# Four fused layers on one core: the last attention steps in a written order, retention's last row factor on GpSimd, the first rows by tile

## What is computed

```python
x = x + tanh(g_xattn[0]) * retention(ln(x), ctx, ctx)      # relu(x@wg) * groupnorm(...) @ wo
x = x + tanh(g_ffn[0])   * moe(ln(x))                      # top 2 of 8 experts + shared, gelu
x = x + tanh(g_xattn[1]) * attention(ln(x), ctx)           # fp8-rounded projections, self + context
x = x + tanh(g_ffn[1])   * dense(ln(x))
# dense:
shared_out = relu(x @ W_up.T) @ W_down.T
rw = softmax(top_k(x @ W_gate.T, 2))
out = shared_out + sum(rw) * (x @ W_expert)
```

## Time and profile before

| | |
|---|---|
| median of 3 executions | 1713.87 us (1713.71 to 1713.95) |
| the profiled execution | 1714.87 us, its span 1713.1 us |
| TensorE busy | 1630.4 us, 95% of the span |
| ScalarE, VectorE, GpSimd busy | 1102.9, 1081.3, 480.9 us |
| mean granted TensorE clock | 0.989 of full speed |
| DMA | 219.67 MB, mean 128 GB/s |

### The profile page before, as it was taken

How to read it: one execution, slowest core, us unless ns; L and a number is a source line. 1 busy time by engine, 2 the same in 40 slices (tenths; PEclk the granted TensorE clock), 3 DMA queues, 4 the chain that set the end, 5 groups by cost and what they waited for, 6 DMA issues and landing times.

```text
span 1713.1 us, 27138 instructions
## 1 busy us (share of the span) xinstructions
PE 1630.4 (95%) x9136; PEld 1337.7 (78%) x9136; DVE 1081.3 (63%) x2117; ACT 1102.9 (64%) x2974; POOL 480.9 (28%) x511
## 2 busy tenths in 40 slices
PE   6989779999998999999999999999999999998998
PEld 5888656666777778888788888788888788876887
DVE  6158854444876667777777776666666666786322
ACT  3454235543657888888888888878777878873100
POOL 1000122223424233433433433333443333420000
PEclk9999889999999999999999999999999999999999
DMA  6120649885663133364343353121151221100011
GB/s 242 49 80 34 266 138 315 299 287 168 235 237 125 50 127 145 113 265 164 113 152 130 127 225 117 57 86 55 56 233 56 69 79 55 56 25 1 25 37 37
DMA packets 74820, 219.67 MB, mean 128 GB/s; under 512 B 6288, under 2 KB 14480, under 8 KB 68304
## 3 DMA queue, kind: packets, MB, share of 16 engines
q1 hardware_dynamic: 69024, 199.56, 32.0%
q0 software_dynamic: 5680, 18.62, 3.5%
HBM read 157.60 MB, written 60.56 MB: 127 GB/s over the span
## 4 chain that ended last, share of the span: by engine, by line
PE 71%; ACT 5%; DVE 5%; DMA 4%; issue 1%; POOL 1%; another core or an unknown queue 0%; POOLq 0%; ACTq 0%; DVEq 0%
PE bank L2377 9%; PE bank L2378 9%; PE bank L97 7%; PE bank L98 7%; PE bank L99 7%; PE bank L2456 6%; PE bank L2438 6%; PE bank L2469 6%; PE bank L2427 5%; DMA s_rows<-x_rows,t_tok 4%; PE bank L2448 3%; PE bank L1349 3%; PE bank L1369 3%; ACT t_sc L2577 1%; ACT t_y L2615 1%
## 5 line engine op out<-in xcount | busy, mean ns | idle before, releaser
L2680 DVE TENSOR_TENSOR t_hn<-bank,t_rs 128x256 f32<-128x256 f32 (+1 forms) x256 | 130.8, 552 | 137.2 <-POOL t_rs L2342 70.4
L2377 PE MATMUL bank<-t_slot,t_x_q 128*128 128x512 f32 x512 | 205.5, 401 | 0.0
L2339 POOL TENSOR_SCALAR t_ve<-t_ss 128x4 f32<-128x4 f32 (+1 forms) x128 | 25.9, 202 | 628.6 <-DVE t_ss L2676 619.4
L2378 PE MATMUL bank<-t_slot,t_x_q 128*128 128x512 f32 x512 | 200.1, 391 | 0.0
L2577 ACT ACTIVATE t_sc<-bank,t_mx 128x128 f32<-128x128 f32 x512 | 183.9, 455 | 3.5 <-DVE t_mx L2700 3.5
L2342 POOL TENSOR_TENSOR t_rs<-t_ve,t_mhalf 128x4 f32<-128x4 f32 (+1 forms) x128 | 171.0, 1336 | 10.6
L2577 ACT ACTIVATION_READ_ACCUMULATOR t_sc<-bank,t_mx 128x1 f32 x512 | 151.6, 296 | 0.0
L2615 ACT ACTIVATE t_y<-bank,smooth 128x128 bf16<-128x128 f32 x512 | 139.2, 399 | 2.1 <-PE bank L2456 2.1
L2438 PEld LDWEIGHTS bank<-t_hT 128*128 128x128 f32 x1024 | 120.9, 192 | 15.8 <-ACT t_hT L2604 15.0
L2438 PE MATMUL bank<-t_hT 128*128 128x128 f32 x1024 | 131.4, 281 | 1.6 <-ACT t_hT L2604 1.6
L2377 PE MATMUL bank<-t_slot,t_x_kv 128*128 128x256 f32 x512 | 125.3, 283 | 2.1 <-DVE x_res L1647 1.4
(11 more groups left out here) (326 smaller groups left out, 4160.1 us busy)
## 6 DMA issues: line engine op xcount, KB each, us to landing
t_xh<-xq_scratch SPq DMA_DIRECT2D x64, 512.0 KB, 3.6
t_slot<-w_ready SPq DMA_DIRECT2D x16, 2048.0 KB, 8.4
t_cr<-in_ctxT_dram SPq DMA_DIRECT2D x64, 256.0 KB, 2.7
y_rows<-s_y SPq DMA_DIRECT2D x39, 256.0 KB
e_w<-in_w_units_dram SPq DMA_DIRECT2D x8, 1024.0 KB, 11.5
w_rows<-in_w_qkv_dram SPq DMA_DIRECT2D x8, 1024.0 KB, 7.2
w_ready<-w_hi SPq DMA_DIRECT2D x8, 1024.0 KB
w_ready<-w_lo SPq DMA_DIRECT2D x8, 1024.0 KB
```

The lines of the kernel that those rows point to most:

```text
L2377: nc.tensor.matmul(out, x_in[:, k, :], w[0][:, k, a:b], start=k == 0, stop=False)
L2378: last = nc.tensor.matmul(out, x_in[:, k, :], w[1][:, k, a:b], start=False, stop=k == KT - 1)
L2680: nc.vector.tensor_tensor(hn[:, lo:hi, :], b3[bk][:, 0:hi - lo, :], rs[:, lo:hi].unsqueeze(2).broadcast_to([P, hi - lo, P]), ALU.mult).the ...
```

## The change

Three parts.

**A.** Chunk 0 of x is loaded as four tiles with a semaphore each, ahead of the parameters; VectorE measures each tile as it lands; TensorE's first turn goes tile by tile instead of group by group; VectorE writes low(0) before statistics(1).

**B.** Three tiles of chunk 3 are measured before the last addition of retention; GpSimd makes the factor of chunk 3 as it does for the others; low(2) moves ahead of the barrier; the root and reciprocal behind it are gone.

**C.** `step` no longer carries Dense's pieces of steps 63 to 66 on TensorE, ScalarE and VectorE; each gets a `last_steps()` with everything written in one order. In `Dense.tensor` the first expert rows come ahead of logits(0), the second ahead of the turned logits(0), and only the second waits for the last row of x; VectorE's first four lines of `Dense.vector` move into `last_steps`.

```diff
-def tile_statistics(nc, env, dve, stats, count, tiles):
+def tile_statistics(nc, env, dve, stats, count, tiles, done=0):
-    for t in tiles:
+    for t in tiles[done:]:
         nc.vector.bn_stats(...)
...
 # Retention.sync
+        for j in range(J):
+            sp.dma_start(env.x_res[:, j, :], dram["x"][j]).then_inc(self.tile_in[j], 16)
         sp.dma_start(env.par[:], dram["params"]).then_inc(self.par_in, 16)
-        rows(0)
...
 # Retention.tensor
+        def first_turn():
+            for j in range(J):
+                pe.wait_ge(self.normed, j + 1)
+                for k in range(KT):
+                    last = nc.tensor.transpose(bank[k][:, ramp(j)], self.xn[0][:, j, ramp(k)], env.ident[:])
+                    if j == J - 1:
+                        last.then_inc(self.turned, 1)
-        turn(0)
+        first_turn()
...
 # Retention.vector
+                for j in range(J):
+                    dve.wait_ge(self.tile_in[j], 16)
+                    v.bn_stats(env.st[:, j, :], env.x_res[:, j, :]).then_inc(self.stats, 1)
...
+        low(0)
         statistics(1)
-        low(0)
         normalise(1)
...
 # Values.gpsimd
-        for c in range(C - 1):
+        for c in range(C):
             pool.wait_ge(self.final, (c + 1) * 2 * J)
             so.row_factors(pool, c)
 # Values.vector, projected(c)
+                if c == 3 and j == 2:
+                    dve.wait_ge(self.x_in, c * J + j + 1)
+                    for t in range(c * J, c * J + J - 1):
+                        v.bn_stats(env.st[:, t, :], env.x_res[:, t, :]).then_inc(self.final, 1)
...
+            if c == C - 1:
+                so.low(dve, 2)
 # Sorting.vector
-        v.tensor_scalar(self.var[:, 0:J], env.mv[:, last_rows, 1], LN_EPS, None, ALU.add).then_inc(self.var_in, 1)
-        dve.wait_ge(self.roots, 1)
-        v.reciprocal(env.rstd[:, last_rows], self.root[:, 0:J]).then_inc(self.rs_in, 1)
         self.normalise(dve, 3, range(J))
-        self.low(dve, 2)
...
 # Dense.expert
         if n == 0:
             pe.wait_ge(self.wlo, self.n["expert"])
+        if n == 1:
             pe.wait_ge(self.rows_in, Q * B)
 # Dense.tensor
+        self.expert(pe, 0, 0)
         self.logits(pe, 0)
-        self.expert(pe, 0, 0)
+        self.expert(pe, 0, 1)
         self.turn_logits(pe, 0)
-        self.expert(pe, 0, 1)
...
 # attention, tensor
+        def last_steps():
+            pe.wait_ge(n_in, M * 4 - 2)
+            de.turn(pe, 0, range(2))
+            turn_probs(M - 2)
+            output(M - 4, M % 2, M * 2 - 2, None)
+            de.turn(pe, 0, range(2, KT))
+            attend(M - 2, M % 2)
+            turn(M - 1)
+            de.turn(pe, 1, range(2))
+            scores(M - 1)
+            de.turn(pe, 1, range(2, KT))
+            de.up(pe, 0, 0)
+            de.up(pe, 0, 1)
+            turn_probs(M - 1)
+            output(M - 3, 1 - M % 2, M * 2, None)
+            attend(M - 1, 1 - M % 2)
+            de.up(pe, 0, 2)
+            output(M - 2, M % 2, M * 2, None)
+            de.up(pe, 0, 3)
+            de.turn(pe, 2, range(2))
+            output(M - 1, 1 - M % 2, M * 2, None)
+            de.turn(pe, 2, range(2, KT))
...
 # attention, scalar
+        def last_steps():
+            exps(M - 2)
+            squares_b(M - 1)
+            de.x_hi(act, 0, range(2))
+            probs_out(M - 2)
+            de.x_hi(act, 0, range(2, KT))
+            heads_out(M - 1)
+            de.x_hi(act, 1, range(2))
+            scaled_out(M - 2, None)
+            exps(M - 1)
+            de.relu(act, 0, 0)
+            de.x_hi(act, 1, range(2, KT))
+            de.relu(act, 0, 1)
+            probs_out(M - 1)
+            scaled_out(M - 1, None)
+            de.relu(act, 0, 2)
+            de.high(act, "expert", 0, KT)
+            de.relu(act, 0, 3)
...
 # attention, vector
+        def last_steps():
+            maxima(M - 2)
+            de.normalise(dve, 1, range(J))
+            probabilities(M - 2)
+            sums_b(M - 1)
+            de.x_lo(dve, 0, range(2))
+            rounded(M - 3, 1 - M % 2, 0)
+            normalise_b(M - 1)
+            de.x_lo(dve, 0, range(2, KT))
+            rounded(M - 3, 1 - M % 2, 1)
+            residual(M - 4, None)
+            de.x_lo(dve, 1, range(2))
+            maxima(M - 1)
+            de.statistics(dve, (10, 11))
+            de.aggregate(dve, 2)
+            probabilities(M - 1)
+            de.h_low(dve, 0, 0)
+            de.x_lo(dve, 1, range(2, KT))
+            rounded(M - 2, M % 2, 0)
+            de.h_low(dve, 0, 1)
+            rounded(M - 2, M % 2, 1)
+            residual(M - 3, None)
+            de.statistics(dve, (12, 13))
+            de.normalise(dve, 2, range(J))
+            rounded(M - 1, 1 - M % 2, 0)
+            de.h_low(dve, 0, 2)
+            rounded(M - 1, 1 - M % 2, 1)
+            residual(M - 2, None)
+            de.low(dve, "expert", 0, KT)
+            de.h_low(dve, 0, 3)
+            de.x_lo(dve, 2, range(2))
+            residual(M - 1, None)
+            de.x_lo(dve, 2, range(2, KT))
+            de.statistics(dve, (14, 15))
+            de.aggregate(dve, 3)
```

More of the change, by code:

```diff
@@ L871, in __init__ @@
         self.tiles = [sb(f"tiles{i}", [P, 4 + E]) for i in range(3)]
-        self.var, self.root, self.dif, self.e1, self.s1 = (sb(n, [P, B]) for n in ("var", "root", "dif", "e1", "s1"))
+        self.dif, self.e1, self.s1 = (sb(n, [P, B]) for n in ("dif", "e1", "s1"))
         self.graw, self.posf, self.slot, self.row, self.ids = (
@@ L889, in __init__ @@
         self.same, self.picked = mem.at("r_same", 170, [P, self.N, E]), mem.at("r_picked", 171.25, [P, self.N, E])
-        (self.wg_in, self.wg_hi, self.wg_lo, self.var_in, self.roots, self.normed, self.turned, self.hi_in, self.lo_in,
+        (self.wg_in, self.wg_hi, self.wg_lo, self.normed, self.turned, self.hi_in, self.lo_in,
          self.lps, self.lsb, self.tps, self.lg_in, self.dif_in, self.e1_in, self.made, self.pad_in, self.scan_in, self.sort_ps,
@@ L894, in __init__ @@
              ctx.enter_context(nc.semaphore("r_" + n)) for n in (
-                 "wg_in", "wg_hi", "wg_lo", "var_in", "roots", "normed", "turned", "hi_in", "lo_in", "lps", "lsb", "tps",
+                 "wg_in", "wg_hi", "wg_lo", "normed", "turned", "hi_in", "lo_in", "lps", "lsb", "tps",
                  "lg_in", "dif_in", "e1_in", "made", "pad_in", "scan_in", "sort_ps", "at_in", "b2_raw_in", "b2_hi_in",
@@ L1046, in scalar @@
         nc, env = self.nc, self.env
-        act.wait_ge(self.var_in, 1)
-        nc.scalar.activation(self.root[:, 0:J], self.var[:, 0:J], ACT.Sqrt).then_inc(self.roots, 1)
         def logits_out(c):
@@ L1889, in after_maxima @@
             self.aggregate(dve, 1)
-        if at == -1:
-            self.normalise(dve, 1, range(J))
     def after_residual(self, dve, at):
@@ L1905, in after_residual @@
             self.statistics(dve, (8, 9))
-        if at == -1:
-            self.x_lo(dve, 0, range(2, KT))
-            self.statistics(dve, (10, 11))
-            self.aggregate(dve, 2)
-            self.x_lo(dve, 1, range(2))
-        if at == 0:
-            self.statistics(dve, (12,))
-            self.h_low(dve, 0, 2)
-            self.h_low(dve, 0, 3)
-            self.normalise(dve, 2, range(J))
-        if at == 1:
-            self.statistics(dve, (13,))
-            self.x_lo(dve, 2, range(2))
-        if at == 2:
-            self.statistics(dve, (14,))
     def logits(self, pe, c):
@@ L2100, in vector @@
     def vector(self, dve):
-        self.statistics(dve, (15,))
-        self.aggregate(dve, 3)
-        self.x_lo(dve, 2, range(2, KT))
-        self.low(dve, "expert", 0, KT)
         self.normalise(dve, 3, range(J))
@@ L2202, in side, with steps @@
         return slice((1 - part) * QH, (1 - part) * QH + QH)
-    def steps(eng, step):
+    def steps(eng, step, end=M - 1):
         for i in range(B + FIRST):
@@ L2214, in steps @@
                     step(v * 2 + (first + 1), (FIRST + 1) % 2, quarter)
-            for i in range(first + 2 * loops, first + B):
+            for i in range(first + 2 * loops, min(first + B, end)):
                 step(i, i % 2, None)
@@ L2365, in gpsimd @@
         rstd(0, 0)
-        steps(pool, step)
+        steps(pool, step, M + FIRST)
         de.rstd(pool, 2)
@@ L2513, in tensor @@
         steps(pe, step)
+        last_steps()
         de.tensor(pe)
@@ L2620, in step @@
                 exps(i - 1)
-            if number(i) == M - 1:
-                de.x_hi(act, 0, range(2))
-            if number(i) == M:
-                de.x_hi(act, 1, range(2, KT))
-                de.relu(act, 0, 0)
             if has(i):
@@ L2632, in step @@
                 probs_out(i - 1)
-            if number(i) == M - 1:
-                de.x_hi(act, 0, range(2, KT))
-            if number(i) == M:
-                de.relu(act, 0, 1)
             if has(i):
@@ L2644, in step @@
                 scaled_out(i - 1, quarter)
-            if number(i) == M - 1:
```

(12 more changed lines are left out.)

42 lines of the change are left out of this document (12 added, 30 removed).

## The result

The changed kernel takes 1695.63 us (1692.54 to 1699.67, 4 executions) against 1713.91 us for the kernel before on the same chip (1713.71 to 1717.81): a ratio of 0.9889, 95% interval 0.9864 to 0.9915, or 19.0 us less where 14.5 were forecast. It is faster, as forecast. But 0.9889 of the first median is 1694.9, and the range ended at 1695.0: the gain was 0.1 us larger than the range allowed. The profiled execution is the shortest of the four, 1692.54 us with a span of 1690.8 us.

A forecast was written before the change was run, and what follows sets the result against it. TensorE, nearly always busy, was taken as the bound, gaining only where it waits or runs slowly, mainly start and tail. Profiled 1714.87 minus 3.6 plus 0.1 minus 11.0 gives 1700.4; less 1.0 to the median, 1699.4 us; range 1695.0 to 1704.5.

The forecast's parts named there:

- rival 2: Start: TensorE's full clock comes early and stays, so the start gains 2 us more, 1697.4 in all; chance 0.14.
- Rival 3: Start: split loads land one after another (1702.0), or low halves stick behind GpSimd's operation (1702.8); chance 0.12.
- the table load: Start: ScalarE loads the root's table in 1.28 us, costing 0.6, with no added drain of about 1.38.
- the two forecast: Tail: new TensorE waits of 0.7 us each, for ScalarE's heads at scores(63) and VectorE's first low half of chunk 3.
- the term for TensorE's busy time: Tail: half clock loses 3.3 us, of which 3.0 counted as winnable because a part coincides with waiting.
- its bound of 12.0: Tail: the most the new order of the last steps was expected to gain, in us; the lower bound was 8.0.
- my two ways of working it out: Tail gain: 11.8 us of waits and clock less 1.4 gives 10.4; walking the lists gives 11.6; middle taken, 11.0.
- the walk through the lists: Tail: five instruction lists, each instruction at its measured length; turn(3) 12.3 us earlier, less 0.7, gives 11.6.
- Rival 1: Tail: VectorE becomes the bound, with 33.6 us of work in 39; 3 us lost, 1702.4 in all; chance 0.18.
- rival 5: Tail: now without gaps, it is granted half clock; slower beyond 29 us of it, 1722 at 45; chance 0.03.
- the last sentence of the sum: Middle of the kernel: the start's gain passes through undiminished, as every wait there is on something that shifts too.
- the 11.0 of C: Tail: forecast gain in us from reordering the last steps, the middle between 10.4 and 11.6.

The follow-up runs named there:

- after: The changed kernel with all three parts, first measurement and profile, against the kernel before: 1695.63 us, ratio 0.9889.
- after_again: The changed kernel run once more with nothing altered: 1696.14 us, ratio 0.9900 to the kernel before.
- part_a: The kernel before with only the change to the first rows at the start: 1707.09 us, ratio 0.9965 to the kernel before.
- old_vector: The changed kernel with VectorE alone back in its old order in the last steps: 1711.22 us, ratio 0.9994 to the kernel before.
- old_tensor: The changed kernel with TensorE alone in its old order in the last steps and Dense's first chunk: 1704.16 us, ratio 0.9951 to the kernel before.
- extra_copies: The changed kernel plus 15 unread 1 MB DRAM copies issued by SyncE in the routed stage: 1721.63 us, ratio 1.0049 to the kernel before.
- best: The changed kernel with first-chunk projections each waiting only for their own low half, and three Dense.tensor pieces moved later: 1692.97 us, ratio 0.9880 to the kernel before.
- staggered: best with prepared weights' low half stored a slot after the high half and next rows loaded a slot later: 1688.77 us, ratio 0.9877 to the kernel before.
- part_b: The kernel before with only the change at retention's end: 1712.32 us, ratio 1.0001 to the kernel before.
- one_load: The changed kernel with its first four tiles in one 1 MB load instead of four: 1696.05 us, ratio 0.9901 to the kernel before.

## Why the prediction was right, and where it was wrong

**Part A was right in size, in part by luck.** The forecast had tiles at 3.5 to 6.5, the parameters at 6.9, rows from 8.85, the projection at 16.05; measured are 3.61 to about 6.25, 6.44, 8.41 and 15.81. One link of the chain was wrong. The transposed weights came at 7.10, not 7.67, and the turn ended at 12.46, not 13.4, but ScalarE was not free then: it had waited for `wg` to land. In all six profiles with this start the projection follows the start of that weight split by 5.1 to 5.3 us. The early steps and the late `wg` nearly cancelled. Over the profiles, the first projection is at 19.60 in the four kernels with the old start and at 16.26 in the six with the new one as it is (after, after_again, part_a, old_vector, old_tensor, extra_copies), and the scan begins at 207.49 and 203.84 in the mean: 3.65 us for A, with 3.6 forecast. The scan of the six lies between 202.76 and 205.85, so this is good to about 1 us, and the first pair's 4.97 is at the upper end. Of rival 2 a little is true. In after the full clock did come at the turn's end, at about 12.0, but went back to half at 15.4, until 18.9. The first twelve products took 4.25 us where they took 4.98 before, and in the mean of the profiles 4.6 in the six and 4.8 in the four: 0.2 us, not 2. Only in best and staggered, whose first projection starts at 14.08 and 13.48, did the full clock stay.

**Rival 3 did not come.** The low halves ran at their normal 0.62 us each beside `wg_lo`, and four loads landed like one: the last of four tiles was there by 6.25, where its statistics start, and one load of all four at 6.18. The Trainium skill ("DMA: Bandwidth & Descriptors", Rules for kernel authors) would have many small transfers coalesced. In this case neither is shown to be better: four loads of 256 KB landed like one of 1 MB, put the load of `wg` 1.3 us later into the queue, and the scan begins as early either way. Of the table load, this trace agrees with the one before and not with the page: the root starts at 7.96, the load ended at 7.94, and the drain that the Trainium skill ("ScalarE: Activation LUTs", What ACT_TABLE_LOAD costs) adds is not there.

**Part B was right.** Counted from the start of the first logits, ahead of the barrier, which is this line in the kernel before and then in the changed one,

```profile
187.63 0.48 PE L107 MATMUL bank<-b_xThi,r_wg 128*128 128x512 f32 x1
```

```profile
182.78 0.48 PE L107 MATMUL bank<-b_xThi,r_wg 128*128 128x512 f32 x1
```

the barrier is released after 3.92 us instead of 3.31, 0.6 later where 0.65 was forecast, the rows behind it start after 3.9 instead of 4.0, and the third logits after 12.03 instead of 12.15: 0.1 us won where 0.1 lost was forecast, inside the bounds. part_b's ratio is 1.0001.

**Part C had the right mechanism and one term too small.** The waits went from 8.76 to 1.38 us, and the two that stay are the two forecast, of 0.70 and 0.68 against 0.7 each. turn(3) starts 12.6 us nearer to Dense's first turn, and 12.3 was forecast. The step that failed is the term for TensorE's busy time, "a part coincides with waiting, so 3.0". The busy time fell by 3.97 us: the clock's loss was 3.2 to 3.4, hardly any of it hidden in waits, and some 0.7 went with the waits themselves, for which the sum had no term. And the profile on which the sum rests is the best of the old tails: with the old order it is 177.26 there, and 178.33 to 178.42 in the three others, whose mean clock is 0.97 rather than 0.98, with 10.2 us at half clock rather than 6.8. In the mean C is 178.10 less 165.71, 12.4 us, above its bound of 12.0. The lower of my two ways of working it out (10.4) was the worse one; the walk through the lists gave 11.6, and I moved away from it. Rival 1 did not come: VectorE was busy for 34.9 of the 40 us from 1518 to 1558 and held TensorE up once in the tail, for 0.68. Nor did rival 5: the tail ran at 1.00.

**The step that made the range too narrow** is the last sentence of the sum, "shifts by A pass through the middle of the kernel, as every wait there is on something that shifts with it". The middle does not only shift. Its routed stage took 180.7 to 185.7 us in twelve profiles of the same code for it, and TensorE's wait for gathered rows goes with it, 8.6 to 12.2; more traffic lengthened both, and in the one profile with spread traffic both were shorter. The profile of the kernel before has the longest stage of all but extra_copies, the profile after one of the shortest. Attention varies by up to 3.9 us, with the clock: the runs whose trace shows no half clock between 411 us and the tail are the short ones (part_a, part_b, old_vector, best, staggered: 1117.0 to 1117.9), and the others, with 3.4 to 10.2 us of it, take 1118.5 to 1120.9. So in the first pair 5.9 us, which the sum put at nothing, came from these two stages.

What is shown adds up to 3.65 and 12.4, 16.1 us. The whole kernel's two ratios give 19.0 (14.6 to 23.3) and 17.1 (14.4 to 19.9). These agree with 16.1. From the scan to the tail it is 1320.9 us in the mean of the four profiles with the old start (1318.6 to 1323.3) and 1318.7 in six with the new one, one_load among them and extra_copies not (1315.2 to 1321.1), so a gain of the middle of some 2 us can't be told from its spread. Whether the remaining 1 to 3 us are chance or a small gain of the middle stays open, and so does why part_a alone gave 6.0 (3.8 to 8.1) and not 3.65. That the time came out just beyond the range is itself within the spread: the second ratio, 0.9900, gives 1696.7 us, inside it. What was too small for certain is the 11.0 of C.

## What to carry to other kernels

When two engines hand work to each other at the end of a pipeline, first look at the order of the engine whose results come late: here the new order of TensorE without VectorE's was worth nothing, while without TensorE's some 5 (by the times) to 9 (by the profile) of 12.4 us stayed. Where gaps go, count the half clock at its full loss, and expect the busy time to shrink a little beyond it. Before a load is split, look at what stands behind it in the queue: here the later `wg` took back what the early tiles had won, as far as the profiles tell. And before a sum is made against one profile, ask which of its stages would look the same in another one: a stage that waits for transfers which meet others needs a spread of its own in the range.

## What the runs showed of the hardware that was not expected

- A gather of 128 rows takes 3.3 us from issue to landing at best, 6.1 at the median and 8.1 at most in the changed kernel, and up to 11.3 where 15 MB more cross its path.
- Waits and clock go together: with more waits in the routed stage the mean clock fell from 0.99 to 0.93, so that the stage grew by 30 us where its waits grew by 18. In the tail, 8.2 to 10.3 us of waits came with 6.8 to 10.2 us at half clock, in five profiles; in the nine with 0.7 to 4.2 us of waits there was none.
- A VectorE tensor_tensor that reads a bank takes 0.62 us (four in 2.48) beside a tensor_tensor of GpSimd of 4.53 us, as without it (four in 2.47).
